# Second projection of the nodes moved into the first aggregation, in a graph, expert and slice-attention kernel

## The reference

```python
te = relu(edge_attr @ We0 + be0) * exp(x @ Wo0 + bo0)[src][:, None]
x = relu(_gat(x, s2, d2, ea2, Wg0, as0, ad0, Wge0, ae0, bg0, n, 4, 64) + x)
te = relu(edge_attr @ We1 + be1) * exp(x @ Wo1 + bo1)[src][:, None]
x = _gat(x, s2, d2, ea2, Wg1, as1, ad1, Wge1, ae1, bg1, n, 1, 256) + x
```

## Time and profile before

| what | us |
|---|---|
| median of 3 runs | 3084.19 |
| lowest, highest | 3080.08, 3086.61 |
| profiled execution | 3083.39 |
| its span on the core | 3081.6 |
| TensorE (PE) busy in the span | 2219.2 (72%) |
| VectorE (DVE) busy | 1816.3 (59%) |
| ScalarE (ACT) busy | 928.1 (30%) |
| GpSimd (POOL) busy | 1070.2 (35%) |

### The profile page before, as it was taken

The page is one execution under the profiler, slowest core; times in us unless marked ns, Lnnn a source line. Parts: engine busy times, 40 slices in busy tenths (PEclk is TensorE's granted clock), DMA queues, the critical chain, the costliest instruction groups (busy, mean ns, idle before and its releaser), DMA issues. The chain is left out here.

```text
span 3081.6 us, 40433 instructions
## 1 busy us (share of the span) xinstructions
PE 2219.2 (72%) x11685; PEld 1644.1 (53%) x11685; DVE 1816.3 (59%) x4267; ACT 928.1 (30%) x1605; POOL 1070.2 (35%) x1034
## 2 busy tenths in 40 slices
PE   5385665336886464528887559964999999998877
PEld 1132454114664353215555447753888888887556
DVE  6498598766775466636776424447644444434754
ACT  5442100121111010210000002226666666664422
POOL 0000276775787436757777443202000000000000
PEclk9797877668999775769999769986999999999977
DMA  4123584334544445435565559942665656552001
GB/s 177 14 110 124 170 268 130 109 111 130 147 137 142 131 163 173 127 104 156 157 168 151 150 207 373 327 120 68 168 152 130 161 132 157 139 150 64 1 15 45
DMA packets 372203, 435.79 MB, mean 141 GB/s; under 512 B 48623, under 2 KB 326224, under 8 KB 368822
## 3 DMA queue, kind: packets, MB, share of 16 engines
q1 hardware_dynamic: 273738, 228.39, 25.0%
q0 software_dynamic: 50496, 151.74, 16.9%
q10 hardware_dynamic: 47808, 53.73, 5.2%
HBM read 336.86 MB, written 97.72 MB: 141 GB/s over the span
## 5 line engine op out<-in xcount | busy, mean ns | idle before, releaser
L665 POOL DMA_INDIRECT gat_ring<-hx_rows,src_i x784 | 832.2, 1061 | 312.7 <-issue 233.4
L2244 PE MATMUL hop_sums<-hop_pieces,hop_weights 128*128 128x512 f32 x3125 | 714.3, 391 | 66.1 <-DVE hop_pieces L2132 65.8
L2244 PEld LDWEIGHTS hop_sums<-hop_pieces,hop_weights 128*128 128x128 f32 x3125 | 589.5, 189 | 190.8 <-DVE hop_pieces L2132 67.5
L2181 ACT ACTIVATE hop_weights<-col_columns 128x640 fp32r<-128x640 f16 x625 | 458.8, 739 | 225.4 <-PE hop_sums L2244 202.8
L1679 PE MATMUL agg_acc<-gat_ring,agg_oh 128*128 x976 | 258.4, 408 | 75.7 <-DVE agg_oh L1588 73.3
L1679 PE MATMUL agg_acc<-agg_msg,agg_oh 128*128 x976 | 248.1, 404 | 78.7 <-DVE agg_oh L1591 78.5
L1679 PEld LDWEIGHTS agg_acc<-gat_ring,agg_oh 128*128 128x128 f32 x976 | 176.2, 196 | 152.9 <-issue 134.3
L1679 PEld LDWEIGHTS agg_acc<-agg_msg,agg_oh 128*128 128x128 f32 x976 | 181.0, 196 | 142.3 <-issue 115.2
L2301 POOL IOTA slc_valid<- 128x25 f32 x1 | 0.2, 162 | 735.1 <-POOLq L76 735.1
L1588 DVE TENSOR_SCALAR agg_oh<-agg_nodes,dst_f,w_cols 128x128 f32<-128x128 f32 x488 | 174.4, 405 | 121.8 <-PE agg_acc L1679 59.3
L814 PE MATMUL look_bank<-look_pieces,look_part 128*128 128x125 bf16 (+1 forms) x2352 | 152.6, 235 | 99.7 <-DVE look_part L769 53.2
(11 more groups left out here) (451 smaller groups left out, 2983.1 us busy)
## 6 DMA issues: line engine op xcount, KB each, us to landing
col_columns<-count_rows SPq DMA_DIRECT2D x60, 1600.0 KB, 8.0
look_part<-src_low SPq DMA_DIRECT2D x28, 896.0 KB, 5.5
exp_w<-in_L_ffn_w SPq DMA_DIRECT2D x16, 1024.0 KB, 11.8
count_windows<-cnt_out SPq DMA_DIRECT2D x67, 200.0 KB, 1.9
count_windows<-cnt_out ACTq DMA_DIRECT2D x64, 200.0 KB, 1.9
gat_ring<-hx_rows,src_i POOLq DMA_INDIRECT x784, 3.2
staged<-gat_ring ACTq DMA_DIRECT2D x14, 520.0 KB
gat_ring<-staged SPq DMA_DIRECT2D x14, 520.0 KB, 3.9
```

What stands on the lines that cost most here:

```text
L665: pool.indirect_dma_start(out=self.ring[:, 4 * slot + 2 * (q % 2) + k, :], out_offset=None, in_=self.g.hx_rows, in_offset=bass.IndirectOff ...
L2181: act.activation(weights[:, q % SLOTS_W, :, :], columns[n % STAGES][:, c * GROUP:(c + 1) * GROUP, b % 2 * P:(b % 2 + 1) * P], ACT.Copy).th ...
L2244: mm = pe.matmul(sums[m % BANKS][:, :], weights[:, q % SLOTS_W, i, :], pieces[k % 2][:, t, :], start=(t == 0), stop=(t == NB - 1))
```

## The change

`project_nodes` is no longer called for layer 1. A new class `NextRows` does its work inside `aggregate` of layer 0, three blocks behind (LAG = 3): TensorE transposes block b - 3 out of the tile y behind the own-rows matmul of block b and multiplies it behind the closing matmul; ScalarE copies the transposed rows, then, one block later, copies the product into a row tile and `sums` and stores the row on its own DMA queue. The rows go into a second table, `hx_next`, since the first is still being gathered from; before layer 1's stages the name `hx_rows` is set to it. The five weight transfers go on ScalarE's queue ahead of its first loads. VectorE makes the weight tile behind block 0's finish. The output tiles y become four, and VectorE's finish also waits for the transpose of the block that last used its tile. At the end stand the three last blocks and the per-node tables. In the diff, cut to its core:

```diff
+class NextRows:
+    LAG = 3
+    H = HEADS[1]
+    W = D + 2 * H + 1
+    def __init__(self, s, g):
+        self.g = g
+        self.w, self.wo, self.bo = s.sb("w", [P, 2, self.W]), s.sb("wo", [P, 2]), s.sb("bo", [P, 1])
+        self.a_row, self.prod = s.sb("a_row", [P, 2, D]), s.sb("prod", [P, D])
+        self.xt = [s.sb(f"next_xt{i}", [P, 2, P]) for i in range(2)]
+        self.full = [s.sb(f"row{i}", [P, ROW]) for i in range(2)]
+        self.sums = s.sb("sums", [P, NB, 2 * self.H + 1])
+        self.turned = [s.ps(f"next_turned{i}") for i in range(2)]
+        self.prod_ps = [s.ps(f"prod_ps{i}") for i in range(2)]
...
+    def load(self, eng, io):
+        nm = lambda n: io[f"L0_gnn_{n}1"]
+        eng.dma_start(self.w[:, :, 0:D], nm("Wg").rearrange("(p k) n -> p k n", p=P)).then_inc(self.given, 16)
+        eng.dma_start(self.wo[:, :], nm("Wo").rearrange("(p k) -> p k", p=P)).then_inc(self.given, 16)
+        eng.dma_start(self.a_row[:, 0, :], across(nm("as").rearrange("h f -> (h f)"), D)).then_inc(self.given, 16)
+        eng.dma_start(self.a_row[:, 1, :], across(nm("ad").rearrange("h f -> (h f)"), D)).then_inc(self.given, 16)
+        eng.dma_start(self.bo[:, :], across(nm("bo"), 1)).then_inc(self.given, 16)
+    def weights_on_vector(self, dve):
+        H = self.H
+        dve.wait_ge(self.given, after(80))
+        link = Linked(dve, self.linked)
+        for k in range(2):
+            for c in range(2):
+                link(dve.tensor_tensor(self.prod[:, :], self.w[:, k, 0:D], self.a_row[:, c, :], ALU.mult))
+                link(dve.tensor_reduce(self.w[:, k, D + c * H:D + (c + 1) * H],
+                                       self.prod[:, :].rearrange("p (h f) -> p h f", h=H), AX, ALU.add))
+        link(dve.tensor_copy(self.w[:, :, self.W - 1], self.wo[:, :]))
+        link(dve.memset(self.full[0][:, :], 1.0))
+        link(dve.memset(self.full[1][:, :], 1.0))
+        dve.sem_inc(self.ready, 1)
+    def turn_on_tensor(self, pe, c, y, whole):
+        pe.wait_ge(whole, after(c + 1))
+        if c >= 2:
+            pe.wait_ge(self.t_copied, after(c - 1))
+        for k in range(2):
+            mm = pe.transpose(self.turned[c % 2][:, k * P:(k + 1) * P], y[:, k:D:2], self.g.ident[:, :])
+        mm.then_inc(self.t_done, 1)
+    def product_on_tensor(self, pe, c):
+        pe.wait_ge(self.t_copied, after(c + 1))
+        if not c:
+            pe.wait_ge(self.ready, after(1))
+        if c >= 2:
+            pe.wait_ge(self.m_read, after(c - 1))
+        for k in range(2):
+            mm = pe.matmul(self.prod_ps[c % 2][:, 0:self.W], self.xt[c % 2][:, k, :], self.w[:, k, :], start=(k == 0),
+                           stop=(k == 1))
+        mm.then_inc(self.m_done, 1)
+    def copy_on_scalar(self, act, c):
+        act.wait_ge(self.t_done, after(c + 1))
+        if c >= 2:
+            act.wait_ge(self.m_done, after(c - 1))
+        act.activation(self.xt[c % 2][:, :, :].rearrange("p k n -> p (k n)"), self.turned[c % 2][:, 0:2 * P],
+                       ACT.Copy).then_inc(self.t_copied, 1)
+    def row_on_scalar(self, act, c):
+        act.wait_ge(self.m_done, after(c + 1))
+        act.wait_ge(self.kept[c % 2], after(16 * (c // 2)))
+        act.activation(self.full[c % 2][:, 0:D], self.prod_ps[c % 2][:, 0:D], ACT.Copy)
+        act.activation(self.sums[:, c, :], self.prod_ps[c % 2][:, D:self.W], ACT.Copy).then_inc(self.m_read, 1)
+        act.wait_ge(self.m_read, after(c + 1))
+        act.dma_start(self.g.hx_next[c * P:(c + 1) * P, :], self.full[c % 2][:, :]).then_inc(self.kept[c % 2], 16)
+    def tables_on_vector(self, dve):
+        H = self.H
+        dve.wait_ge(self.m_read, after(NB))
+        dve.memset(self.g.small_sb[:, :, :], 0.0).then_inc(self.split, 1)
+        dve.wait_ge(self.split, after(1))
+        dve.tensor_copy(self.g.small_sb[:, :, 0:H], self.sums[:, :, 0:H])
+        dve.tensor_copy(self.g.node_d[:, :, 0:H], self.sums[:, :, H:2 * H]).then_inc(self.split, 1)
+    def tables_on_scalar(self, act):
+        act.wait_ge(self.split, after(2))
+        act.activation(self.g.small_sb[:, :, 4], self.sums[:, :, 2 * self.H], ACT.Exp, bias=self.bo[:, 0:1]
+                       ).then_inc(self.tabled, 1)
+        act.wait_ge(self.tabled, after(1))
+        for i in range(2):
+            act.wait_ge(self.kept[i], after(16 * len(range(i, NB, 2))))
 def aggregate(nc, g, io, layer, out_dram):
@@ -1469,10 +1565,11 @@
-        YS = 8 if layer else 2
+        YS = 8 if layer else 4
         y = [s.sb(f"y{i}", [P, D]) for i in range(YS)]
         rows = RouteRows(s, g) if layer else None
-        lag, group = RouteRows.LAG, RouteRows.GROUP
+        following = None if layer else NextRows(s, g)
+        lag, group = RouteRows.LAG if layer else NextRows.LAG, RouteRows.GROUP
...
@@ -1504,6 +1601,8 @@
                 act.dma_start(bias[:, :], across(io[f"L0_gnn_bg{layer}"], D)).then_inc(consts, 16)
                 if layer:
                     rows.load(act, io)
+                else:
+                    following.load(act, io)
@@ -1549,6 +1648,12 @@
                         load(b + 1)
                     if layer and b >= lag:
                         rows.copy_on_scalar(act, b - lag)
+                    if not layer and b > lag:
+                        following.row_on_scalar(act, b - lag - 1)
+                    if not layer and b >= lag:
+                        following.copy_on_scalar(act, b - lag)
+                if not layer:
+                    following.row_on_scalar(act, NB - 1 - lag)
                 store(NB - 2)
                 if layer:
                     rows.root_on_scalar(act, NB // group - 1)
@@ -1557,6 +1662,11 @@
                     for c in range(NB - lag, NB):
                         rows.copy_on_scalar(act, c)
                     rows.all_kept(act)
+                else:
+                    for c in range(NB - lag, NB):
+                        following.copy_on_scalar(act, c)
+                        following.row_on_scalar(act, c)
+                    following.tables_on_scalar(act)
@@ -1612,6 +1722,8 @@
                     sums = heads(acc[i][:, 0:R])
                     dve.wait_ge(summed, after(b + 1))
                     dve.wait_ge(stored[b % YS], after(16 * (b // YS)))
+                    if not layer and b >= YS:
+                        dve.wait_ge(following.t_done, after(b - YS + 1))
                     link(dve.reciprocal(inv[i][:, :], sums[:, :, F]))
                     if layer:
                         dve.scalar_tensor_tensor(out, acc[i][:, 0:D], inv[i][:, 0:1], base, ALU.mult,
@@ -1648,12 +1760,16 @@
                         finish(b - 1)
                     if b and layer:
                         route_rows(b - 1)
+                    if b == 1 and not layer:
+                        following.weights_on_vector(dve)
                     if b + 1 < NB:
                         dve.wait_ge(numbered, after(b + 2))
                         first, last = last, visit(last, b + 1, False, lambda: last_quad(dve, b + 1))
                 finish(NB - 1)
                 if layer:
                     route_rows(NB - 1)
+                else:
+                    following.tables_on_vector(dve)
@@ -1669,6 +1785,8 @@
                     pe.matmul(sums, g.ident[:, :], looped[b % 2][:, :], start=True, stop=False, skip_group_check=True)
                     if layer and b >= lag:
                         rows.turn_on_tensor(pe, b - lag)
+                    if not layer and b >= lag:
+                        following.turn_on_tensor(pe, b - lag, y[(b - lag) % YS], turned_up)
                     last = last_quad(pe, b)
                     with pe.Fori(first, last + 1) as q:
                         moving = at(ring, q % HELD) if layer else at(msg, q % 2)
@@ -1683,7 +1801,15 @@
                               skip_group_check=True).then_inc(summed, 1)
                     if layer and b >= lag:
                         rows.gate_on_tensor(pe, b - lag)
+                    if not layer and b >= lag:
+                        following.product_on_tensor(pe, b - lag)
                     first = last
+                if not layer:
+                    following.turn_on_tensor(pe, NB - lag, y[(NB - lag) % YS], turned_up)
+                    for c in range(NB - lag, NB):
+                        if c + 1 < NB:
+                            following.turn_on_tensor(pe, c + 1, y[(c + 1) % YS], turned_up)
+                        following.product_on_tensor(pe, c)
@@ -2618,7 +2744,7 @@
-        g.hx_rows, g.src_low, g.src_high = dram("hx_rows", [NP, ROW]), dram("src_low", [EP], F16), dram("src_high", [EP], F16)
+        g.hx_rows, g.hx_next, g.src_low, g.src_high = dram("hx_rows", [NP, ROW]), dram("hx_next", [NP, ROW]), dram("src_low", [EP], F16), dram("src_high", [EP], F16)
...
@@ -2648,7 +2774,7 @@
             project_nodes(nc, g, io, 0, io["x"], True)
             for layer, target in enumerate((g.x_mid, g.x_gnn)):
                 if layer:
```

(11 more changed lines are left out.)

## The result

The changed kernel takes **3027.9 us** (median of 4 runs, 3025.2 to 3029.5); the kernel before took 3082.1 beside it (4 runs, 3078.8 to 3086.6). The ratio is 0.9822, with a 95% interval of 0.9805 to 0.9839. The profiled execution took 3029.49 us with a span of 3027.7, 53.9 less than the 3083.39 of before. The forecast was 3040 with 3032 as the lower end: the sign and the place of the gain were right, the gain was ten us larger, and the time lies outside the range.

The account below looks back on a forecast made before the run. POOL's gather issue was taken to bound the first aggregation. Gain: 59.7 - 10.0 - 1.0 - 2.8 - 0.2 - 0.8 - 1.0 = 43.9 us, giving 3040 us, with a range of 3032 to 3053.

Parts of the forecast that it names:

- The bound: First aggregation: POOL's gather issue is full from first gather to last; VectorE and TensorE have 40.5 us of slack.
- What is removed: Second projection's stage, from its first load's issue to the next stage's first transfer: 59.7 us saved.
- The start: Start of first aggregation: five transfers ahead of ScalarE's first loads make POOL begin 2.8 us later (ends 2 and 5).
- The loop: TensorE's two transposes and product in 22 blocks, plus VectorE's weights: up to 38 of 40.5 us slack, 0 on the path.
- The weights on VectorE: First aggregation: four added products of two SBUF tiles may lengthen gathers, 0 to 1.7 us, taken as +1.0.
- The last block: Last block of the aggregation: 1.43 us of added TensorE work delays its first quad, taken as +0.8 us.
- The tail: After the last sum: three remaining blocks put the last store's issue 10.0 us later (ends 8 and 13.5).
- 1.0 for the clock: Tail: +1.0 us in all for TensorE's lower clock level, at which each of three products costs 1.06 more.
- The boundary felt in full (1): Loop's block boundaries and start: added work felt in full, worse start, handshake losses, some 12 us excess, 3052; chance 0.15.
- the chain exposed in every block (2): Loop: transpose, copy, product exposed at 2.75 us per block, some 29 us over, 3068; chance 0.06.
- Dearer gathers by stores (3): First aggregation's gathers lengthened by row stores and ScalarE's traffic, 32 us slower, 3116; chance 0.03.
- More than forecast (4): Start and tail at lower ends (2 and 8), no cost of clock and weights: 49 us gained, 3035; chance 0.14.

Follow-up runs that it names:

- the meetings taken away: Kernel before, with VectorE first copying the first aggregation's edge weights into PSUM, so its product of messages reads one SBUF input: 3045.2 us, ratio 0.9877.
- the doubled product: Changed kernel, with TensorE's product of the second projection done twice in each block of the loop: 3036.6 us, ratio 0.9847.
- the run with the stores alone: Kernel before, with three ScalarE copies and one store of rows per block on dummy data, nothing on TensorE: 3086.2 us, ratio 1.001.
- the other order: Changed kernel, weight transfers behind block 1's own rows, ScalarE's copies one block ahead of rows, block 23's store ahead of row 21: 3019.1 us, ratio 0.9790.

## Why the prediction was right or wrong, by its steps

- **The bound** (POOL's gathers, full from the first to the last): right. It is full again, and with the meetings taken away from the kernel before, 48 us of the stretch and some 38 of the time went. **What is removed** (59.7): right; no stage stands between the first aggregation and the look-up.
- **The start** (2.8, and 0.2 for semaphores): 1.3. No run shows the 0.2; the stage's first transfer was issued at 710.08 before and at 709.92 with the change, so nothing came in its place. The price of the weight tile's issue was read from a queue that had five loads ahead of it (1.68); here, on another engine's queue and with one small load ahead of it, it took 0.65. The own rows were used 2.4 us later (716.65 against 714.26), and a part of that was hidden behind VectorE's first product, which stood in the way before as well.
- **The loop** (0, out of a slack of 40.5): right. The wait for SyncE came down to 13.6, inside the 5 to 30 that were named, and with the doubled product 12 us more of it were used before the stage's end moved with it. Of the 26.9 us that the slack lost, 8.8 are the faster gathers, so the added work took some 18.
- **The weights on VectorE** (+1.0 in the gathers): *this is the step that failed*. It priced new meetings alone, four small products, and put the cost between 0 and 1.7, so it excluded a gain without a reason. Of the four, one met a gather, and that one took 1.15 (at 742.56): 0.2 us is what they cost. The row that it used (1.51 beside the product at 1044.42) already told that a gather's length depends on when it starts against a product, and the 0.22 between the mean of 1.17 and the median of 0.948 is 50 us over the stage. Work on TensorE moves VectorE's one-hot tiles and with them all the products (VectorE waited 72 times for TensorE to be done with such a tile, before 56 times). The gathers took 8.8 us less. This error of 9.8 is nearly the whole 10 by which the sum missed.
- **The last block** (+0.8): 2.4. The forecast had only the work at the boundary. That accounts for 1.0: TensorE comes to the last block's first quad behind a product (1.12) and two transposes (0.40), and VectorE's last two products stand 2.80 us apart (1043.90 and 1046.70) instead of 1.83 (1049.95 and 1051.78). The other 1.5 was not forecast at all. VectorE had waited 3.15 us for a landing, TensorE idled for 3.58 and did the quad at the lower clock, in 3.60 instead of 2.02, so that VectorE's last but one product starts 4.64 us behind the last gather instead of 3.16. With the 1.7 too much at the start the two nearly cancel.
- **The tail** (10.0 and 1.0 for the clock): 10.9 were measured. But two of three products ran at the lower level, 2.0 us instead of 1.0, and the rest was 1 less than worked out. The last store stood 12.7 behind the last sum, where 11.7 and the 1.0 for the clock were forecast.
- **The rivals.** The boundary felt in full (1) and the chain exposed in every block (2) did not come: the only waits for the copy are the three in the tail. Dearer gathers by stores (3): 2 us in the trace of the run with the stores alone, where it needed 0.2 us for each gather. More than forecast (4) had the right sign and the wrong cause: the start was below its lower end, but the tail was not, and the gathers gave what it did not have.

The Trainium skill (SBUF — State Buffer, Who interferes with whom) says that a VectorE instruction with two inputs in SBUF contends with a GpSimd instruction that reads SBUF, and that one with at most a single SBUF input, outside VectorE's 2-port modes, does not. The runs agree with both: 50 us of excess with the weights in SBUF, 1 with them in PSUM. The prediction priced such meetings for the added instructions and not for those that were there.

What stays open: how to tell beforehand which spacings of the products a change will leave. The rows show that the spacing sets the cost, and that TensorE's added work moved products from 0.6 to 1.5 us behind the one before; no run set the spacing by itself. In every run that gave TensorE more work the gathers grew cheaper (a mean of 1.167 to 1.120 and to 1.127, and 1.127 to 1.097), and none shows the opposite. By the rule above a spacing just under 1.12 or 2.37 us would cost 1.1 for each product, so that a change could also cost time is an estimate from it, and not shown.

## What to carry to other kernels

When the engine that bounds a stage has two lengths of one instruction, the difference between mean and median times the count is a cost that a change beside it can move (here it fell by 7 to 10 us each time that TensorE got more work; that it can rise was not shown): put it into the range, or take it away first by giving the other engine's instruction an input outside SBUF. Read a moved issue's price from a row on the same queue with the same work ahead of it; which of the two made the 1.68 of before was not tested. And in a tail that a pipeline leaves behind, order the work so that TensorE is not left waiting between products, for here the wait cost twice, by itself and by the clock.

## What the runs showed of the hardware that was not expected

An indirect gather that starts during VectorE's product of two SBUF tiles ends 0.82 us behind the product's end (0.81 to 0.83 in all 182 pairs of the two kernels whose gather took over 1.0 us), whatever its start up to 0.13 us before that end; one that has started before the product keeps its 0.95 (a median of 0.946 over 126 of them). The product itself keeps its 1.24 in both cases. So the spacing of the products alone gives what each meeting costs, within 0.1 us for 179 of 186. Two transposes and a product per block that do nothing made a kernel 0.3% faster (0.9957 to 0.9983) by that alone. And in the tail of the change, where TensorE had paused 1.16, 0.95 and 1.38 us before its three last products, the last two took 2.09 and 2.10 us, at a granted clock of 0.50; in the other order, with pauses of 0.91, none and 0.23, they took 1.14, 1.08 and 1.14.
